# Key maxima rows transferred in step 7, query rows behind step 1's diagonal keys, the queries' bias sums behind the first convolution half

## The chip, the cores and the metric
The kernel runs on one core of a Trainium2 chip. The time is the device time of one execution in microseconds (us). TensorE (PE), VectorE (DVE), ScalarE (ACT) and GpSimd (POOL) run their own instruction streams and meet at semaphores; the sync engine (SP) issues nearly all the DMAs, in one queue and in the order of its program.

## The reference
One decoder layer on 8 sequences of 128 tokens with 128 channels, in float32:

```
x = x + attn1(layernorm(x))        # 16 heads of 8 channels; queries and keys pass a 3-tap
                                   # convolution and a projection of [input, convolved input];
                                   # scores * tau + delta, softmax over 128 keys, times V, out
x = x + attn2(layernorm(x), ctx, mask)   # 16 heads, keys and values from ctx, masked softmax
x = x + moe(layernorm(x))          # 64 experts, 8 of them per token, and one shared expert
```

In `attn1` the projection and the convolution are folded: `Q3 = conv(q_in) @ qp2 + q_in @ qp1` becomes one convolution over the normalised input, with a bias column that sums `qp2 @ convq_b` and three taps applied to the query bias. The same holds for the keys.

## The kernel before, in words
**Head.** The input is normalised (DVE), turned to channels-by-tokens on PE (`turn_inputs`, two halves of four sequences), copied to `xnT` by ACT, and convolved on PE (`convolve`, line 531, one half at a time). `sum_bias` (line 524) is eight small float32 matmuls with one output column: two passes each for four products. `sum_bias(0, ...)` (queries) stands between the two `turn_inputs`, `sum_bias(1, ...)` (keys) behind the first half's convolution. DVE applies the results in `foldb` (line 1240).

**Stacked operands.** The attention multiplies float32 numbers as two float32r parts, high and low. For each of 16 heads the parts are stacked on 32 partitions: rows 0 to 7 of such a block are for the running maximum (`S_MAX = 8`), rows 8 to 31 hold the eight channels times three parts. The stacked keys are `kst[0]` (first attention) and `kst[1]` (second), the stacked queries `qst`. Sequences 0 to 3 are stacked by PE (`stack`, line 495) and evicted by ACT and DVE. Sequences 4 to 7, and the keys of the second attention, go through DRAM: `put_rows(i, ...)` (line 376, three DMAs of 256 KB, or 512 KB for i = 2) stores the parts, `get_rows` (line 382, four DMAs) reads them back in stacked order. The maxima rows of the keys are constants: ACT writes them for sequences 4 to 7 of `kst[0]` (`fill_keys`, signal `kst_filled`), and `get_maxima(lo)` (line 388) copies them by four DMAs from `kst[0]` to `kst[1]`, 8 partitions to 8 partitions, 64 KB each. It is called for lo = 0 and lo = 4: eight DMAs, signal `maxima_got`.

**Steps.** There are 16 steps (`STEPS`), one for each sequence in each attention. In a step PE computes the scores of 16 heads in four groups against `kbd`, a block-diagonal copy of that sequence's keys with two buffers. DVE takes the maxima (`maximum`, line 1295) and splits them (`split_max`), PE turns them (`turn_max`, L656 and L659), ACT and DVE write `qbd`, PE computes the transposed scores, ACT the exponentials, PE the product with the values. PE runs one step ahead with `scores`. In steps 7 and 11 `scores(s + 1, 0)` stands late, between the groups of `scoresT(s)`, because the queries of the second attention are made there (`second_stack`).

**The SP queue** (lines 358 to 477). Behind the loads: wait for `kst_filled`, `get_maxima(0)` and `(4)`, wait for the split keys, `put_rows(0)`, wait for the split queries, `put_rows(1)`. Then a loop over s = 1 to 15: wait for the keys' source (`kst_ready`, `rows_got`; from s = 8 also `maxima_got`), wait until step s - 2's scores are read (`scored`), four DMAs that write `kbd` for step s (line 439), `move_rows(s)` (line 395: the `get_rows` of later sequences, `put_rows(2)` at s = 6, `get_rows(2)` at 7 and 9), and loads of expert weights (line 370; five of 192 KB at s = 8). POOL also waits for `maxima_got` before it splits the weights of pairs 5 to 9 (line 1846), behind step 7's exponentials.

Of the kernel before, what the change touches and what calls it, by code (L numbers as in the profile page):

```python
# [19 lines left out]
G = 4  # L20
# [10 lines left out]
Q_PARTS, K_PARTS = (0, 1, 0), (0, 0, 1)  # L31
# [30 lines left out]
def decoder_layer(nc, x, ctxT, mask, pack_a, pack_b, w3, rowsd, outT):  # L62
# [3 lines left out]
    with ExitStack() as ctx:  # L66
# [3 lines left out]
        def sem(name):  # L70
            return ctx.enter_context(nc.semaphore(name))
# [51 lines left out]
        qhl = by_part("qhl")  # L123
# [96 lines left out]
        qhi_ready = sem("qhi_ready")  # L220
        qlo_ready = sem("qlo_ready")
# [7 lines left out]
        kst_filled = sem("kst_filled")  # L229
# [105 lines left out]
        def wait(eng, signal, value):  # L335

            if not isinstance(value, int) or value > 0:
                eng.wait_ge(signal, value)
# [17 lines left out]
        @block.sync  # L356
        def _(sp):
            sp.dma_start(xres[:, :, :], x.rearrange("(b p) d -> p b d", p=P)).then_inc(ld_x, 16)
            nf = cols_a[FOLD_LAST][1]
            sp.dma_start(pa[:, 0:nf], pack_a[:, 0:nf]).then_inc(ld_f, 16)  # L360
            sp.dma_start(pa[:, nf:n_a], pack_a[:, nf:n_a]).then_inc(ld_a, 16)
            sp.dma_start(ctxs[:, :, :], ctxT.rearrange("p (b t) -> p b t", b=B)).then_inc(ld_ctx, 16)
            sp.dma_start(pb[:, :], pack_b).then_inc(ld_b, 16)
            sp.dma_start(masku[:, :, :], mask.rearrange("b q k -> q b k")).then_inc(ld_mask, 16)
            w3v = w3.rearrange("p (n m c) -> p n m c", m=3, c=P)
            def load(pair):

                if pair >= RING:
                    sp.wait_ge(wlo_ready, pair + 1 - RING)
                sp.dma_start(ring[:, pair % RING, :, :], w3v[:, pair, :, :]).then_inc(ld_w[pair % RING], 16)  # L370

            for pair in range(RING):
                load(pair)


            def put_rows(i, hl, first, parts):

                for m, a in enumerate(parts):
                    sp.dma_start(split_rows[i, :, m, P * first:T],  # L379
                                 hl[:, a, first:B, :].bitcast(F32).rearrange("p b t -> p (b t)")).then_inc(rows_put[i], 16)  # L380

            def get_rows(i, st, lo, hi, quarters):
                src = split_rows[i].rearrange("(g j d) m t -> j (d m) g t", g=G, j=J)
                for j in quarters:
                    sp.dma_start(st[32 * j + S_MAX:32 * j + 32, :, lo:hi, :].bitcast(F32).rearrange("p g b t -> p g (b t)"),
                                 src[j, :, :, P * lo:P * hi]).then_inc(rows_got[i][lo // 2], 16)

            def get_maxima(lo):

                for j in range(J):  # L390
                    sp.dma_start(kst[1][32 * j:32 * j + S_MAX, :, lo:lo + 4, :].bitcast(F32).rearrange("p g b t -> p g (b t)"),  # L391
                                 kst[0][32 * j:32 * j + S_MAX, :, 4:B, :].bitcast(F32).rearrange("p g b t -> p g (b t)"))\
                        .then_inc(maxima_got, 16)

            def move_rows(s):

                if s == 2:
                    sp.wait_ge(rows_put[0], 48)
                    get_rows(0, kst[0], 4, 6, range(J))
                if s == 3:  # L400
                    sp.wait_ge(rows_put[1], 48)
                    sp.wait_ge(qst_cleared, 1)
                    get_rows(1, qst, 4, 6, range(J))
                if s == 4:
                    get_rows(0, kst[0], 6, B, range(J))
                if s == 5:
                    get_rows(1, qst, 6, B, range(J))
                if s == 6:
                    sp.wait_ge(khi_ready, 4)
                    sp.wait_ge(klo_ready, 4)  # L410
                    put_rows(2, khl[1], 0, K_PARTS)
                if s == 7:
                    sp.wait_ge(rows_put[2], 48)
                    get_rows(2, kst[1], 0, 4, range(J))
                if s == 9:
                    get_rows(2, kst[1], 4, B, range(J))

            sp.wait_ge(kst_filled, G)
            get_maxima(0)
            get_maxima(4)  # L420
            sp.wait_ge(khi_ready, 2)
            sp.wait_ge(klo_ready, 2)
            put_rows(0, khl[0], 4, K_PARTS)
            sp.wait_ge(qhi_ready, 2)
            sp.wait_ge(qlo_ready, 2)
            put_rows(1, qhl, 4, Q_PARTS)
            sp.wait_ge(rows_ready, 3)
            for s in range(1, STEPS):
                n, b = s // B, s % B
                if s < 4:  # L430
                    sp.wait_ge(kst_ready, G)
                elif s < B:
                    sp.wait_ge(rows_got[0][2 if s < 6 else 3], 64)
                else:
                    sp.wait_ge(rows_got[2][b // 4 * 2], 64)
                    sp.wait_ge(maxima_got, 128)
                wait(sp, scored, G * (s - 1))
                for j in range(J):
                    sp.dma_start(kbd[32 * j:32 * j + 32, s % 2, :, j, :].bitcast(F32),
                                 kst[n][32 * j:32 * j + 32, :, b, :].bitcast(F32)).then_inc(kbd_ready[s % 2], 16)  # L440
                move_rows(s)
                for pair in PAIR_LOADS.get(s, ()):
                    load(pair)

            def coefficient_rows(n):

                c = n // PER_HALF
                sp.wait_ge(gate_scaled, n + 1 - ROWS)
                e0 = 2 * (n - PER_HALF * c) - 2
                for r in range(2):  # L450
                    sp.dma_start(spread[I * r:I * r + I, n % ROWS, :, :].rearrange("p b t -> p (b t)"),
                                 rowsd[c, e0 + r:e0 + r + 1, :].broadcast_to([I, HALF])).then_inc(ld_c[n % ROWS], 16)

            def rows_out(c):

                sp.wait_ge(rowsT_copied, c + 1)
                sp.dma_start(rowsd[c, :, :], coef_rows[:, c, :]).then_inc(rows_stored, 16)
                sp.wait_ge(rows_stored, 16 * (c + 1))

            load(EARLY_PAIRS + RING - 1)  # L460
            rows_out(0)
            for n in range(FIRST, UNITS):
                if n == PER_HALF + 1:
                    rows_out(1)
                if n != PER_HALF:
                    coefficient_rows(n)
                if n in load_unit:
                    load(load_unit[n])
                if n == PER_HALF + LAG + ROWS + 2:
                    sp.wait_ge(out_copied, 1)  # L470
                    sp.dma_start(outT[:, 0:HALF], outs[:, 0, :]).then_inc(stored, 16)

            for i in range(2):
                sp.wait_ge(out_copied, i + 2)
                cols = slice(2 * P * i, 2 * P * i + 2 * P)
                sp.dma_start(outT[:, HALF + 2 * P * i:HALF + 2 * P * i + 2 * P], outs[:, 1, cols]).then_inc(stored, 16)
            sp.wait_ge(stored, 48)
# [3 lines left out]
        def _(pe):  # L481
# [3 lines left out]
            def mm(out, lhsT, rhs, start=True, stop=True):  # L485
                return pe.matmul(out, lhsT, rhs, start=start, stop=stop)  # L486

            def turn_inputs(n, c, out):

                for b in range(4 * c, 4 * c + 4):  # L490
                    pe.wait_ge(xn_ready, B * n + b + 1)
                    last = pe.transpose(out[:, P * (b % 4):P * (b % 4) + P], xn[:, b, :], ident)  # L492
                last.then_inc(xT_done, 1)
# [30 lines left out]
            def sum_bias(n, proj, conv_bias, bias):  # L524

                mm(bank[4][:, n:n + 1], A(proj), A(conv_bias), True, False)
                for k in range(3):
                    last = mm(bank[4][:, n:n + 1], folds[n][:, k, :], A(bias), False, k == 2)
                last.then_inc(bias_summed, 1)
# [18 lines left out]
            pe.wait_ge(natural_copied, 1)  # L548
            compose(0)
            turn_inputs(0, 0, bank[0])  # L550
            sum_bias(0, "qp2T", "cqb", "bq")
            compose(1)
            turn_inputs(0, 1, bank[1])
            pe.wait_ge(pads_ready, 2)
# [1 line left out]
            for c in range(2):  # L556
                pe.wait_ge(xT_copied, c + 1)
                pe.wait_ge(compose_copied, c + 1)
                convolve(0, convq, c, bank[5 + c]).then_inc(q_done, 1)
                if c == 0:  # L560
                    sum_bias(1, "kp2T", "ckb", "bk")

            def time_scales():
# [1363 lines left out]
```

## Time and profile before

| | us |
|---|---|
| median of 3 runs | 304.18 (302.94 to 401.68) |
| the profiled execution | 303.79 |
| its span (first to last instruction) | 302.0 |
| PE busy | 288.7 (96%) |
| DVE, ACT, POOL busy | 228.2, 191.3, 185.3 |

The span is what the profiler covers; 1.8 us of the profiled execution lie around it. PE is busy nearly all the time, but a matmul's end is modelled, and a busy PE can run at half clock. The profile divides the span in 40 slices of 7.55 us. "L439" is line 439 of the kernel; SPq is a DMA issue on the sync engine; matmuls issued by a helper all have the helper's line, L486. A DMA share is the mean busy share of 16 DMA engines.

### The profile page before, as it was taken

What the parts mean: (1) busy time and instruction counts of PE and PEld (TensorE: products, weight loads), DVE (VectorE), ACT (ScalarE), POOL (GpSimd) and SP (SyncE); (2) the same over time, 40 slices, a digit from 0 to 9 for tenths busy, and PEclk for the clock granted to TensorE, in tenths of its full rate; (3) what the DMA queues carried; (4) which work ended last, traced back from release to release, by engine and by line L of the source; (5) the groups of instructions that cost most, each with busy time, mean ns of one, the idle gap of its engine ahead of it and who ended that gap; (6) DMA issues with size and microseconds to landing.
All of it is one profiled execution on the core that took longest, in us unless ns stands there. A gap on an engine that the chain in (4) does not pass through costs nothing.

```text
span 302.0 us, 5440 instructions
## 1 busy us (share of the span) xinstructions
PE 288.7 (96%) x1721; PEld 206.3 (68%) x1721; DVE 228.2 (76%) x513; ACT 191.3 (63%) x352; POOL 185.3 (61%) x259
## 2 busy tenths in 40 slices
PE   8999979999999999899889999999999999999995
PEld 3654756666655565456665788888888888888883
DVE  3698877799859886987896559789956676676664
ACT  2698827796884666466752797766655555555553
POOL 8430061098708870985177799999975666666661
PEclk9999968999999999999999999999999999999999
DMA  7702764457576243350000637766434353444311
GB/s 260 242 2 31 194 161 101 101 112 258 111 201 124 63 105 95 89 140 2 2 1 25 199 113 205 214 198 188 131 99 137 109 171 126 127 134 131 123 61 35
DMA packets 30636, 37.18 MB, mean 123 GB/s; under 512 B 5136, under 2 KB 19856, under 8 KB 30608
## 3 DMA queue, kind: packets, MB, share of 16 engines
q1 hardware_dynamic: 30608, 36.84, 43.0%
q8 instruction: 14, 0.23, 0.4%
q14 instruction: 14, 0.11, 0.1%
HBM read 28.43 MB, written 3.93 MB: 107 GB/s over the span
## 4 chain that ended last, share of the span: by engine, by line
PE 80%; DVE 10%; SPq 5%; ACT 2%; issue 2%; DMA 1%; ACTq 0%; DVEq 0%
PE bank L486 54%; PE bank L866 5%; PE bank L868 5%; PE bank L867 5%; PE bank L672 2%; SPq L391 2%; PE bank L647 2%; PE bank L690 2%; SPq L379 1%; PE bank L659 1%; DVE conv L1232 1%; DVE conv L1230 1%; PE bank L695 1%; PE bank L492 1%; PE bank L656 1%
## 5 line engine op out<-in xcount | busy, mean ns | idle before, releaser
L1864 POOL TENSOR_TENSOR qbd<-vs,qbd 128x512 fp32r<-128x512 f32 x65 | 83.8, 1291 | 33.3 <-ACT qbd L1175 33.2
L486 PE MATMUL bank<-khl,stacks 128*128 128x512 f32 x396 | 101.5, 392 | 1.9 <-DVE vs L1659 1.9
L486 PEld LDWEIGHTS bank<-khl,stacks 128*128 128x128 f32 x396 | 73.5, 188 | 18.7 <-issue 3.7
L1690 DVE TENSOR_TENSOR conv<-bank,conv 128x512 f32<-128x512 f32 x60 | 41.5, 692 | 31.4 <-ACT bank L1139 28.2
L1139 ACT ACTIVATE bank<-bank 128x512 f32<-128x512 f32 x61 | 35.5, 582 | 43.9 <-PE bank L486 43.9
L1298 DVE TENSOR_REDUCE rawmax<-bank 128x4 f32<-128x512 f32 x64 | 43.3, 684 | 10.9 <-PE bank L486 10.0
L1175 ACT ACTIVATE qbd<-vs 128x512 fp32r<-128x512 f32 x65 | 40.6, 624 | 7.1 <-DVE vs L1667 4.6
L486 PE MATMUL bank<-stacks 128*128 128x512 f32 x96 | 42.2, 488 | 2.8 <-DMA stacks<-stacks 2.0
L1698 DVE TENSOR_TENSOR vs<-conv,bank 128x512 f32<-128x512 f32 x61 | 41.9, 687 | 2.1
L1063 ACT ACTIVATE conv<-bank 128x512 f32<-128x512 f32 x64 | 35.1, 596 | 7.0 <-PE bank L486 6.3
L1828 POOL TENSOR_TENSOR stacks<-ring,stacks 128x384 fp32r<-128x384 f32 x33 | 33.6, 1020 | 1.4
L486 PE MATMUL bank<-qbd,stacks 128*128 128x512 f32 x64 | 30.7, 530 | 0.4 <-ACT conv L1063 0.4
L1072 ACT ACTIVATE qbd<-bank 32x512 fp32r<-32x512 f32 x40 | 23.5, 587 | 11.9 <-PE bank L659 11.6
L866 PE MATMUL bank<-qbd,stacks 128*128 128x512 f32 (+1 forms) x67 | 26.4, 394 | 0.7 <-POOL qbd L1864 0.6
L868 PE MATMUL bank<-qbd,stacks 128*128 128x512 f32 (+1 forms) x67 | 25.9, 386 | 0.0
L867 PE MATMUL bank<-qbd,stacks 128*128 128x512 f32 (+1 forms) x67 | 25.9, 386 | 0.0
L486 PEld LDWEIGHTS bank<-stacks 128*128 128x128 f32 x96 | 18.4, 196 | 8.2 <-DMA stacks<-stacks 2.3
L486 PE MATMUL bank<-conv,vs 128*9 128x128 f32 (+1 forms) x520 | 23.3, 279 | 0.0
L1051 ACT ACTIVATE oT<-bank 128x512 f32<-128x512 f32 x16 | 9.6, 598 | 15.1 <-PE bank L486 15.1
L1834 POOL CAST stacks<-ring 128x384 fp32r<-128x384 f32 x17 | 8.6, 504 | 17.0 <-ACT conv L1063 9.4
L1314 DVE CAST qbd<-bank 32x512 fp32r<-32x512 f32 x24 | 16.7, 694 | 1.6 <-PE bank L659 1.0
L486 PEld LDWEIGHTS bank<-conv,vs 128*9 128x9 f32 (+1 forms) x520 | 12.4, 91 | 7.6 <-issue 5.7
(239 smaller groups left out, 440.9 us busy)
## 6 DMA issues: line engine op xcount, KB each, us to landing
conv<-coefficient_rows SPq DMA_DIRECT2D x122, 128.0 KB, 2.9
ring<-w SPq DMA_DIRECT2D x33, 192.0 KB, 3.6
stacks<-stacks SPq DMA_DIRECT2D x68, 64.0 KB, 2.1
split_rows<-stacks SPq DMA_DIRECT2D x6, 256.0 KB, 3.4
stacks<-split_rows SPq DMA_DIRECT2D x16, 96.0 KB
split_rows<-khl SPq DMA_DIRECT2D x3, 512.0 KB, 4.3
stacks<-split_rows SPq DMA_DIRECT2D x8, 192.0 KB
pa<-pack_a SPq DMA_DIRECT2D x1, 706.0 KB, 5.4
```

Of the source, the lines that this page charges most:

```text
L486: return pe.matmul(out, lhsT, rhs, start=start, stop=stop)
L866: pe.matmul(acc, whi(pair)[:, 2, :], hhi[:, w, cols], start=False, stop=False, skip_group_check=True)
L867: pe.matmul(acc, whi(pair)[:, 2, :], hlo[:, w, cols], start=False, stop=False, skip_group_check=True)
L868: pe.matmul(acc, wlo(pair)[:, 2, :], hhi[:, w, cols], start=False, stop=stop, skip_group_check=True).then_inc(down_done, 1)
L1063: act.activation(probs[:, i % 8, :, :].rearrange("p j t -> p (j t)"), bank[2 + i % 2][:, :], ACT.Exp, scale=SCALE).then_inc(exped, 1)
L1139: act.activation(out, four(2 + p), ACT.Silu).then_inc(silu_done, 1)
L1175: act.activation(hhi[:, n % 4, :].rearrange("p (b t) -> p b t", b=4), hx[n % 4], ACT.Copy).then_inc(hhi_ready, 1)
L1298: dve.tensor_reduce(rawmax[:, s % 2, g, :].unsqueeze(2), bank[i % 2][:, :].rearrange("p (j k) -> p j k", j=J), AX.X, ALU.max, negate=True) ...
L1690: dve.tensor_tensor(out, gate, spread[:, n % ROWS, :, :], ALU.mult).then_inc(gate_scaled, 1)
L1698: dve.tensor_tensor(hx[n % 4], scaled[:, 4 * p:4 * p + 4, :], four(4 + p), ALU.mult).then_inc(h_done, 1)
L1828: pool.tensor_tensor(wlo(pair), ring[:, pair % RING, :, :], whi(pair).bitcast(F32), ALU.subtract).then_inc(wlo_ready, 1)
L1864: pool.tensor_tensor(hlo[:, n % 4, :].rearrange("p (b t) -> p b t", b=4), hx[n % 4], hhi[:, n % 4, :].bitcast(F32).rearrange("p (b t) -> p ...
```

## The change
It has three edits. The eight `get_maxima` DMAs, and the wait for `kst_filled` before them, move from the head of the SP queue into `move_rows(7)`, behind `get_rows(2, kst[1], 0, 4)`. `put_rows(1)` with its waits moves from before the loop to s = 1 of the loop, behind the four `kbd` DMAs. The queries' `sum_bias` moves from between the two input turns to behind the first half of the query convolution, in front of the keys' one.

```diff
@@ move_rows
                 if s == 7:
                     sp.wait_ge(rows_put[2], 48)
                     get_rows(2, kst[1], 0, 4, range(J))
+                    sp.wait_ge(kst_filled, G)
+                    get_maxima(0)
+                    get_maxima(4)
                 if s == 9:
                     get_rows(2, kst[1], 4, B, range(J))
 
-            sp.wait_ge(kst_filled, G)
-            get_maxima(0)
-            get_maxima(4)
             sp.wait_ge(khi_ready, 2)
             sp.wait_ge(klo_ready, 2)
             put_rows(0, khl[0], 4, K_PARTS)
-            sp.wait_ge(qhi_ready, 2)
-            sp.wait_ge(qlo_ready, 2)
-            put_rows(1, qhl, 4, Q_PARTS)
             sp.wait_ge(rows_ready, 3)
@@ loop over s
                                  kst[n][32 * j:32 * j + 32, :, b, :].bitcast(F32)).then_inc(kbd_ready[s % 2], 16)
+                if s == 1:
+                    sp.wait_ge(qhi_ready, 2)
+                    sp.wait_ge(qlo_ready, 2)
+                    put_rows(1, qhl, 4, Q_PARTS)
                 move_rows(s)
@@ tensor engine
             turn_inputs(0, 0, bank[0])
-            sum_bias(0, "qp2T", "cqb", "bq")
             compose(1)
             turn_inputs(0, 1, bank[1])
@@
                 convolve(0, convq, c, bank[5 + c]).then_inc(q_done, 1)
                 if c == 0:
+                    sum_bias(0, "qp2T", "cqb", "bq")
                     sum_bias(1, "kp2T", "ckb", "bk")
```

## Rows read from the trace of the kernel before
**Rows 1.** The page: busy us (share) xinstructions, and the clock in 40 slices.
```profile
PE 288.7 (96%) x1721; PEld 206.3 (68%) x1721; DVE 228.2 (76%) x513; ACT 191.3 (63%) x352; POOL 185.3 (61%) x259
...
PEclk9999968999999999999999999999999999999999
```
**Rows 2.** The chain of waits, 36 to 49 us: start, us, what.
```profile
36.87 1.11 SPq L439
...
39.41 2.09 DMA stacks<-stacks
```
**Rows 3.** Timeline, PE's: start, us, instruction, [idle before <-releaser].
```profile
41.54 0.79 PE L486 MATMUL bank<-stacks 128*128 128x512 f32 x1 [1.98 <-DMA stacks<-stacks]
```
**Rows 4.** Timeline of the SP queue.
```profile
24.86 7.18 SPq L391 DMA_DIRECT2D stacks<-stacks  x8
32.16 4.61 SPq L379 DMA_DIRECT2D split_rows<-stacks  x6
...
73.91 1.56 SPq L385 DMA_DIRECT2D stacks<-split_rows  x4
80.83 2.52 SPq L439 DMA_DIRECT2D stacks<-stacks  x4
83.40 2.51 SPq L370 DMA_DIRECT2D ring<-w  x5
86.02 2.54 SPq L439 DMA_DIRECT2D stacks<-stacks  x4
```
**Rows 5.** Timeline of DVE and ACT, 30 to 36 us.
```profile
30.21 0.75 DVE L1261 SCALAR_TENSOR_TENSOR stacks<-bank,foldb,stacks 128x512 fp32r<-128x512 f32 x1 [0.69 <-ACT stacks L970]
...
34.32 0.69 ACT L974 ACTIVATE stacks<-bank,key_rows 128x512 fp32r<-128x512 f32 x1 [0.23 <-PE bank L486]
```
**Rows 6.** Timeline of DVE, 40 to 49 us.
```profile
40.54 0.19 DVE L1306 TENSOR_TENSOR negmax<-rawmax,negmax 128x16 fp32r<-128x16 f32 x1
...
42.38 0.69 DVE L1298 TENSOR_REDUCE rawmax<-bank 128x4 f32<-128x512 f32 x1 [1.51 <-PE bank L486]
...
48.01 0.19 DVE L1306 TENSOR_TENSOR negmax<-rawmax,negmax 128x16 fp32r<-128x16 f32 x1
```
**Rows 7.** Timeline of PE, 8 to 30 us: a bias sum, the last convolution's end.
```profile
11.14 0.81 PE L486 MATMUL bank<-pa,qin 128*128 128x1 f32 x6
...
28.95 0.50 PE L537 MATMUL bank<-small,kin 128*128 128x4 f32 x4
```
**Rows 8.** Windows: us, busy (count) of PE, PEld, DVE, ACT, POOL, PEclk, DMA share, GB/s.
```profile
26.00:33.00 7.00, 7.00 (x24) 3.66 (x23) 5.67 (x10) 5.83 (x10) 0.00 (x0) 1.00 0.44 65
...
41.00:42.00 1.00, 0.46 (x1) 0.46 (x2) 0.00 (x0) 0.00 (x0) 1.00 (x1) 0.50 0.40 77
...
70.00:72.00 2.00, 2.00 (x11) 1.27 (x10) 1.61 (x7) 1.90 (x5) 1.45 (x7) 1.00 1.02 395
...
76.00:79.00 3.00, 3.00 (x23) 2.06 (x26) 2.55 (x8) 2.66 (x6) 2.29 (x8) 1.00 0.81 158
...
80.00:81.00 1.00, 1.00 (x19) 0.58 (x7) 0.93 (x5) 0.77 (x3) 0.92 (x2) 1.00 0.00 0
...
88.00:92.00 4.00, 3.88 (x19) 2.65 (x19) 3.22 (x7) 2.69 (x6) 0.64 (x2) 1.00 0.73 174
```
**Rows 9.** Line 439 in step 8's, step 9's and step 10's windows: landing times.
```profile
DMA to landing us min/median/max: 2.1/2.1/2.1
...
DMA to landing us min/median/max: 3.0/3.2/3.3
...
DMA to landing us min/median/max: 3.4/3.7/4.0
```
**Rows 10.** Timeline of PE: `scores(8, 0)`, `scores(9, 0)`, step 8's L659.
```profile
88.12 0.38 PE L647 MATMUL bank<-maskb,identb 128*128 128x512 bf16 x1
...
92.44 0.38 PE L647 MATMUL bank<-maskb,identb 128*128 128x512 bf16 x1 [0.36 <-DVE rawmax L1298]
...
93.62 0.51 PE L659 MATMUL bank<-identr,negmax 128*128 128x512 f32 x1 [0.33 <-DVE negmax L1306]
```

## The prediction
> **What bounds the kernel now.** I read the page first: PE is busy 96% of the span, so most of it is PE's own work, and the clock line has one dip, in slices 6 and 7 [rows 1]. The chain of waits for that place runs along the SP queue: eight maxima DMAs, six row stores, then the four `kbd` DMAs of step 1, the last issued at 39.41 and landed 2.09 later [rows 2, 4]. PE, which wants them for `scores(1, 0)`, has been idle for 1.98 us when it starts at 41.54, the one long wait for a DMA in the steps [rows 3]. At 41 us the granted clock is 0.50, that is 1.2 instead of 2.4 GHz [rows 8]. So the reader is to see two things: at 40 us the end is set by the SP queue, elsewhere (step 7 among it) by PE, with SP ahead of it by a margin that has to be read.
>
> **Part 1, the head of the SP queue.** Without the maxima, `put_rows(0)` can issue when the keys' low parts are there, at 30.21 + 0.75 = 30.96 [rows 5], not at 32.16 [rows 4]. Six such DMAs took 4.61 us, so even if most of that falls to these three, they end before 34.3. The `kbd` DMAs then wait for the last stacked keys: 34.32 + 0.69 = 35.01 [rows 5]. They issue at 35.05 instead of 36.87 and at 0.65 each the fourth starts at 37.0; with the observed 2.1 it lands at 39.1, at the slower pace seen (2.54 for three) at 39.7. The old date was 41.50. The supply is 1.8 to 2.4 us earlier.
>
> What is late next is DVE: step 0's maxima are split at 40.54 + 0.19 = 40.73 and nothing in the change touches them. Behind that DVE idled until 42.38, 1.51 us by the row [rows 6]. `scores(1, 0)` would now be ready by 40.2, so this maximum starts at 40.87 and the DVE chain to the next split (at 48.01 before, mostly without holes) moves up by 1.5, plus the 0.2 to 0.4 us of waits for PE in it that the full clock takes out. **Gain: 1.7 us.** Bounds: 0, if the stores in flight slow the four DMAs until 41.5, and 2.4, the whole advance of the supply; I take 1.7 because DVE's own row is nearest. The clock dip should vanish, as PE's hole shrinks from 1.98 to about 0.4 us, but it is worth little here since DVE bounds the stretch.
>
> **Part 2, `put_rows(1)`.** Its three issues (about 1.6 us) come behind step 1's four, 37.7 to 39.3. Behind them queue step 2's `kbd` DMAs, which waited for step 0's scores until about 39.5 anyway. Nothing. If one issue is as slow as the slowest seen, step 2's move by 1 us and are still before PE's next step, which waits for the second split (46.4 after part 1's gain). Its reader, `get_rows(1)`, comes two steps later.
>
> **Part 3, the bias sums.** They are 0.81 us and a bit of PE time [rows 7]. PE works without a hole from there to 29.45, where the last key convolution ends [rows 7], and DVE's low keys, which set the start of the stores and stacks, follow from it: DVE is idle for 0.69 before them [rows 5]. The sums stay within that stretch, so its end does not move; the second input half reaches ACT and DVE 0.8 us sooner, which they spend waiting for PE at its end. Cost and gain nothing; bounds plus or minus 0.8, the sum's own length, if a hole opens or closes.
>
> **Part 4, the maxima in step 7.** All times here are on the old clock; the gain of part 1 moves PE and SP alike. `get_rows(2)` issues from 73.91 to 75.47. Its traffic runs at a share of 0.81 and 158 GB/s and is gone at 80, and step 8's `kbd` DMAs start at 80.83 [rows 4, 8]: 1.0 us from the end of traffic to the next issue. The eight maxima DMAs issue from 75.5. In the old place they took long: first issue 24.86, a share of only 0.44 and 65 GB/s from 26 to 33, 455 of 524 KB by then, so their traffic ended about 34.0 at that pace [rows 4, 8]; a little less is likely, 33.6, as it began after 26. That is some 7.6 us of traffic for half a megabyte, where `put_rows(2)` had 395 GB/s at a share of 1.02 [rows 8]. They are limited by something of their own, and it is not the total rate (the packets are as long as those of the rows, 2 KB).
>
> Step 8 now waits for `maxima_got`. When does it come? Call T the start of step 8's `kbd` issues (80.83 before). If the maxima ran beside the rows with no loss: 75.5 + (33.6 - 24.86) + 1.0 = 85.2. If they run behind them, as step 10's DMAs did, which landed in 3.4 to 4.0 us behind a `get_rows` against 2.1 elsewhere [rows 9]: 79.8 + 6.5 to 7.6 + 1.0 = 87.3 to 88.4 (6.5 is the 7.6 at 0.44 packed to a share of 0.51, half of the full 1.02, about what these copies never passed). If both were spread over all engines with no loss, 0.81 x 4.5 and 0.44 x 7.6 us of work at 1.02 from 75.3 end at 82.1, T = 83.1. I take 87.3; the queueing seen in step 10 is the nearest row.
>
> The Trainium skill (DMA: Bandwidth & Descriptors, section "Why a DMA increments its semaphore by 16 and not by 1") says that a transfer from the sync engine runs on the largest number up to 16 that divides both sides' slowest dimension, and on the lowest-numbered engines: 8 for these 8 partitions. The trace agrees with a share of 0.44 while only the maxima move. By that rule the maxima share every one of their engines with the rows ahead of them, which gives the 87.3; were it wrong, T would be between 83.1 and 85.2.
>
> PE reads step 8's `kbd` at 88.12 [rows 10]. Of four DMAs the last starts 1.95 behind T and lands 2.1 later [rows 9], so T may be 84.07 at most. With T = 87.3 PE waits 3.2 us. Next, SP issues the five weight loads before step 9's `kbd`: their fourth starts at T + 7.15 and lands 3.0 later (it did behind the loads [rows 9]), at 97.45. PE wanted step 9's at 92.44 and could have taken them at 92.9, with L659 waiting for DVE until 93.62 [rows 10]; moved by 3.2 that is 96.1, so 1.3 us more are lost. The other possibility is that the 3.2 us hole brings the clock down, as the 1.98 us one did [rows 3, 8]: then PE's 3.88 busy us of 88 to 92 double, less what DVE's waits give back, 2.5 us, and step 9's wait is covered. One or the other, 1.3 or 2.5; I take the middle, 1.9, as one old hole is all there is to judge by. **Loss: 3.2 + 1.9 = 5.1 us.** POOL also waits for the maxima but was idle until 91.28 for step 7's exponentials. Step 10's DMAs come one step later, with no weight loads between, and SP has caught up by then.
>
> **Sum.** -1.7 + 0 + 0 + 5.1 = +3.4: 303.79 + 3.4 = **307.2 us**. The profiled execution is 0.4 below the median of three.
>
> **Rivals.**
> *The maxima run beside the rows.* T = 85.2: PE waits 1.1 at 88.12 and 1.3 more for step 9, each shorter than the hole that brought the clock down. -1.7 + 2.4 = +0.7: 304.5. For it: the share of 0.81 leaves room; against: 0.81 + 0.44 is more than 1.02, and step 10's landings.
> *The maxima are hidden.* The one that is not slower. Place: `maxima_got` at SP, s = 8; price nothing; it decides at T of about 82.8 (from there step 9's DMAs land by 92.9). It needs the spread of 83.1, or a faster pace than at the head, where DVE and ACT may have been what slowed the copies. With T = 83.1 the loss is 0.3, without any it is none: -1.4 to -1.7, 302.2. Against it: alone they took 9.7 us from first issue to landing, and here 8.0 are given.
> *Slower by over 2%.* T = 88.4 gives a wait of 4.3; the clock falls (2.5 more) and part 1 gives nothing for a slowed issue: 303.8 + 6.8 = 310.6.
> *The early part does not work* (step 1's DMAs still late by stores in flight) with the forecast's loss: 303.8 + 5.1 = 308.9; within the range.
>
> **How the numbers follow.** Two per cent is 6 us, about what a measurement here can tell from no change. Forecast with its neighbour 308.9: 0.53. Beside the rows, 304.5: 0.20. Hidden, 302.2: 0.17. Over 2% slower: 0.08. Over 2% faster needs 6 us where the whole supply gain is 2.4: 0.02. The range takes in the hidden case's value and the forecast with T = 88.4 or without part 1's gain, 302.0 to 309.6.
>
> **What would show it.** In the changed profile PE's wait for a DMA at 41.5 is gone and the clock line has no dip there; L391 stands at about 74; SP waits some 5 to 6 us at line 439 in step 8 and PE has a hole of about 3 us before the first L647, perhaps with a clock of 0.50 behind it. The forecast is wrong if the maxima's landing comes within 8 us of their first issue, or if their rate is well over the 65 GB/s of the head.

## Result: 1.6% slower, and the profile after

| | before | changed |
|---|---|---|
| median, us | 303.91 (4 runs) | 307.75 (4 runs, 307.54 to 310.2) |
| profiled execution, span | 302.0 | 306.0 |

The ratio of the changed kernel to the one before is 1.0156 [1.0087, 1.0224]; 307.2 was forecast. One of the four runs before took 401.68 us; the ratio is of the others, whose median is 303.64. The kernel is slower beyond the interval; a loss of over 2% is not excluded by it. In the two profiled executions the head gained 2.0 us and steps 8 and 9 lost 6.0.

The turned maxima of each step (L659 before, L660 in the changed kernel) serve as milestones: the difference of their starts shows where the time went, to 0.1 us:

| start of it in step | 0 | 1 | 7 | 8 | 9 |
|---|---|---|---|---|---|
| before | 42.56 | 48.26 | 84.08 | 93.62 | 100.06 |
| changed | 40.75 | 46.23 | 82.11 | 97.30 | 104.07 |
| difference | -1.81 | -2.03 | -1.97 | +3.68 | +4.01 |

The span's +4.0 is complete at step 9. Between steps 7 and 8 lie 15.19 us instead of 9.54: 5.65 lost; between 8 and 9 another 0.33.

The SP queue of the changed kernel, from its timeline (start, us, instruction); it answers to [rows 4]:

```profile
30.97 1.29 SPq L379 DMA_DIRECT2D split_rows<-stacks  x3
35.00 2.71 SPq L436 DMA_DIRECT2D stacks<-stacks  x4
37.81 1.52 SPq L379 DMA_DIRECT2D split_rows<-stacks  x3
...
71.36 1.99 SPq L385 DMA_DIRECT2D stacks<-split_rows  x4
73.40 6.96 SPq L391 DMA_DIRECT2D stacks<-stacks  x8
86.17 2.56 SPq L436 DMA_DIRECT2D stacks<-stacks  x4
88.77 2.51 SPq L370 DMA_DIRECT2D ring<-w  x5
91.40 2.54 SPq L436 DMA_DIRECT2D stacks<-stacks  x4
93.98 1.82 SPq L385 DMA_DIRECT2D stacks<-split_rows  x4
95.90 8.33 SPq L436 DMA_DIRECT2D stacks<-stacks  x8
```

The stores start at 30.97 and step 1's keys at 35.00, as worked out. The last maxima DMA is issued at 79.67, step 8's keys only at 86.17. The chain of waits says what stands between (the landing of that last copy), and that step 10's keys were late too:

```profile
79.67 6.44 DMA stacks<-stacks
...
97.82 5.51 DMA stacks<-stacks
```

PE at the three places, from its timeline; the first row answers to [rows 3], the others to [rows 10]:

```profile
39.76 0.77 PE L487 MATMUL bank<-stacks 128*128 128x512 f32 x1 [0.29 <-DVE rawmax L1299]
...
90.29 0.39 PE L648 MATMUL bank<-maskb,identb 128*128 128x512 bf16 x1 [4.28 <-DMA stacks<-stacks]
...
96.34 0.39 PE L648 MATMUL bank<-maskb,identb 128*128 128x512 bf16 x1 [0.54 <-DMA stacks<-stacks]
```

The wait at the head has become one for DVE; the 4.28 us is new. Windows (us, busy of PE, PEld, DVE, ACT, POOL, then clock, DMA share, GB/s), to read beside [rows 8]:

```profile
40.00:41.00 1.00, 1.00 (x3) 0.53 (x4) 0.93 (x5) 0.00 (x0) 0.18 (x1) 0.50 1.00 358
...
76.00:79.00 3.00, 3.00 (x41) 1.91 (x39) 2.87 (x7) 2.50 (x7) 2.42 (x7) 1.00 0.68 120
...
80.00:84.00 4.00, 3.67 (x30) 2.12 (x27) 1.95 (x7) 3.70 (x9) 0.00 (x0) 1.00 0.52 76
84.00:85.00 1.00, 1.00 (x19) 0.52 (x18) 0.90 (x4) 0.47 (x2) 0.00 (x0) 1.00 0.16 20
...
91.00:94.00 3.00, 3.00 (x8) 1.91 (x7) 1.46 (x3) 1.08 (x2) 0.00 (x0) 0.50 0.85 272
```

Once the rows are through, the maxima are alone from 80 to 84: a share of 0.52, 76 GB/s, against 0.44 and 65 at the head before. The first copy is issued at 73.40 and the last has landed at 86.11, 12.7 us later. At 40 us and again from 91 to 94 the clock is at 1.2 GHz.

### The profile page after: what moved, and what is told of

It is laid out like the page before. It is cut to its first block, busy times and chain, and to the rows that moved or that the text cites. A ratio compares the mean times of both kernels' runs of the same rounds, so it can differ in the third digit from the quotient of the medians.

```text
span 306.0 us, 5440 instructions
## 1 busy us (share of the span) xinstructions
PE 289.4 (95%) x1721; PEld 206.3 (67%) x1721; DVE 228.2 (75%) x513; ACT 191.5 (63%) x352; POOL 185.0 (60%) x259
## 4 chain that ended last, share of the span: by engine, by line
PE 71%; DVE 10%; SPq 7%; DMA 7%; issue 2%; ACT 1%; ACTq 0%; DVEq 0%
PE bank L487 48%; PE bank L867 5%; PE bank L869 5%; PE bank L868 5%; DMA stacks<-stacks 4%; SPq L436 3%; PE bank L673 2%; SPq L391 2%; PE bank L648 2%; DVE rawmax L1299 2%; DMA split_rows<-khl 2%; DMA xres<-x 1%; SPq L385 1%; PE bank L691 1%; PE bank L660 1%
## 5 line engine op out<-in xcount | busy, mean ns | idle before, releaser
L1176 ACT ACTIVATE qbd<-vs 128x512 fp32r<-128x512 f32 x65 | 40.7, 625 | 7.1 <-DVE vs L1668 4.6
L648 PE MATMUL bank<-maskb,identb 128*128 128x512 bf16 x32 | 12.7, 396 | 5.3 <-DMA stacks<-stacks 5.0
```

The costliest lines, as they stand in the source:

```text
L1176: act.activation(hhi[:, n % 4, :].rearrange("p (b t) -> p b t", b=4), hx[n % 4], ACT.Copy).then_inc(hhi_ready, 1)
```

## Experiments
Times are medians; "L659" and "L660" are the same matmul in kernels with other line numbers. Experiments 1 to 4, 5 to 8 and 9 to 12 were compared with runs of the kernel before of 303.67, 303.70 and 303.94; every ratio is to that kernel. The diffs are cut to the lines that matter, and some of their comments are not in the kernels. Those of 1, 2, 5, 7 and 8 start from the kernel before, that of 10 starts from experiment 9, of 11 from 4, of 12 from 6, and the others from the changed kernel.

### 1. The maxima's edit alone
```diff
-            sp.wait_ge(kst_filled, G); get_maxima(0); get_maxima(4)   # head of the queue
+                    # in move_rows(7), behind get_rows(2, kst[1], 0, 4)
+                    sp.wait_ge(kst_filled, G); get_maxima(0); get_maxima(4)
```


> The kernel before with the maxima's edit alone: their eight DMAs stand in step 7, the query stores and the bias sum stay where they were. My theory (in step 7 the maxima run behind the row reads, and step 8's key DMAs wait for them) puts the whole loss into this edit, and also the gain at the head: six stores fit between 30.97 and 35.0, so step 1's key DMAs still issue at 35.1 to 35.6. It expects the changed kernel's time, 307.3 to 308.2, a wait of 4 us on PE at 90 us, and L379 x6 ending by 35.6. The rival (the query stores' move carries the head's gain) expects 309 to 310: the loss of 6 without the gain of 2.

308.67, ratio 1.0164 [1.0151, 1.0177]. Loss and head gain are both in this edit: L659 of step 1 stands at 46.27, that of step 8 at 98.65. The six stores were issued by 34.1, in time. It is 0.5 above what I gave, since more is lost at step 8 than in the changed kernel: 7.1 us instead of 5.65. Experiment 9 comes back to that.

### 2. The other two edits, maxima at the head
```diff
             sp.wait_ge(kst_filled, G)
             get_maxima(0)
             get_maxima(4)
             put_rows(0, khl[0], 4, K_PARTS)
-            put_rows(1, qhl, 4, Q_PARTS)
+            # put_rows(1, ...) at s = 1 behind the kbd DMAs; sum_bias(0, ...) behind convolve(0, ..., 0)
```


> The other two edits without the maxima's: maxima stay at the head of the SP queue, the query stores stand behind step 1's key DMAs, the bias sum behind the first convolution half. My theory expects no loss at all at step 8, and a gain at the head, since step 1's key DMAs now issue behind three stores instead of six: at 35.1, 1.8 us sooner than in the kernel before, landing at 39.2 to 40.2. PE's second split moves up by 1.3 to 2.0: 301.9 to 302.6. A rival (the stores' traffic, now in front of step 2's DMAs, costs something or the gain needs the maxima gone, whose traffic still slows the three stores) expects 303.3 to 304.5.

302.09, ratio 0.9963 [0.9947, 0.998]. No loss at step 8 (L660 of steps 7 and 8 are 9.54 apart, as before), and by the times the gain is there. But the runs are of two kinds: eight at 301.66 to 302.27 and four at 303.5 to 303.74. The profile caught one of the latter, and its windows show why:

```profile
14.00:18.00 4.00, 4.00 (x26) 3.04 (x25) 3.56 (x3) 4.00 (x6) 3.99 (x2) 1.00 0.00 0
18.00:21.00 3.00, 3.00 (x5) 1.05 (x4) 2.93 (x6) 2.71 (x4) 0.00 (x0) 0.50 0.03 5
```

From 18 to 21 us PE runs at 1.2 GHz in the middle of the convolutions, with no hole before; what stands before are the two bias sums in a row, eight products of one column each, here 15.1 to 17.0:

```profile
15.12 0.36 PE L487 MATMUL bank<-pa 128*128 128x1 f32 x2
15.34 0.81 PE L487 MATMUL bank<-pa,qin 128*128 128x1 f32 x6
16.01 0.36 PE L487 MATMUL bank<-pa 128*128 128x1 f32 x2
16.24 0.81 PE L487 MATMUL bank<-pa,kin 128*128 128x1 f32 x6
16.91 4.37 PE L487 MATMUL bank<-xnT,oT 128*128 128x512 f32 x6
```

The last row took 2.82 us in the profile of the changed kernel. Step 1's L660 stands at 48.10 instead of 46.23, 1.9 us later.

### 3. The maxima spread over steps 2 to 5
```diff
                 move_rows(s)
+                if s == 2:
+                    sp.wait_ge(kst_filled, G)
+                if 2 <= s < 6:
+                    get_maxima(4 * (s // 4), range(2 * (s % 2), 2 * (s % 2) + 2))
```


> The changed kernel with the eight maxima DMAs in pairs behind the moves of steps 2, 3, 4 and 5 instead of all in step 7. My theory (the loss is only the place: behind the row reads, with 8 us to the wait) expects all maxima landed before 62 us, the SP wait in step 8 back to that for the rows, no PE wait at 88, and the head's gain kept: 301.7 to 302.6. A rival (these copies are slow wherever they stand, and delay the key DMAs queued behind them on the same DMA engines) expects PE waits for a DMA in steps 3 to 6 of together 1 to 3 us: 303 to 305.

306.25 over twelve runs (303.95 to 308.69); ratio, without the two longest (308.64 and 308.69), 1.0077 [1.0052, 1.0103]. My theory fell here, the rival was nearer, though by another mechanism. The SP queue itself became the bound of these steps:

```profile
59.50 1.48 SPq L391 DMA_DIRECT2D stacks<-stacks  x2
61.08 3.15 SPq L433 DMA_DIRECT2D stacks<-stacks  x4
64.27 1.82 SPq L385 DMA_DIRECT2D stacks<-split_rows  x4
66.13 1.48 SPq L391 DMA_DIRECT2D stacks<-stacks  x2
67.71 2.95 SPq L433 DMA_DIRECT2D stacks<-stacks  x4
```

One round takes 6.63 us (59.50 to 66.13) where PE's step takes 6.09, and the key DMAs behind maxima issue at 3.15 instead of 2.52. But from step 1's maxima to step 7's it is only 0.7 us longer than the changed kernel. The profile (306.1) shows two more losses. It has the slow head of experiment 2, 2.1 us at step 1's maxima. And the queue is still late when the copies are through: step 8's keys issue at 84.23, 0.7 us ahead of step 7's maxima, where it was 3.25 before, and PE waits for the keys of steps 9 and 10:

```profile
94.25 0.39 PE L649 MATMUL bank<-maskb,identb 128*128 128x512 bf16 x1 [1.31 <-DMA stacks<-stacks]
...
101.59 0.39 PE L649 MATMUL bank<-maskb,identb 128*128 128x512 bf16 x1 [0.82 <-DMA stacks<-stacks]
```

### 4. The maxima copied by POOL
```diff
+            pool.wait_ge(kst_filled, G)
+            for lo in (0, 4):
+                pool.tensor_copy(kst[1][:, :, lo:lo + 4, :]..., kst[0][:, :, 4:B, :]...).then_inc(maxima_got, 1)
             pool.wait_ge(kbd_first, 1)
```


> The changed kernel without maxima DMAs: POOL copies the constants from the first stacked keys to the second in two instructions of 128x2048, behind ACT's fill at about 25 us, where it was idle until 37. SP waits for them at step 2 and step 7, POOL as before. By its casts of 128x384 in 0.50 us, 2.7 us each, so done by 30.5. My theory expects what the spread one does, and no queue effects: 301.7 to 302.4. The rival (POOL beside DVE slows DVE's long operations between 25 and 31, which set the low parts) expects the stores at 31.5 to 33 instead of 30.97 and 302.5 to 304.

303.97 (303.71 to 305.77), ratio 1.0013 [1.0001, 1.0024]. Step 8 is as before, but the head lost what was gained. The profile is of the slowest of the twelve runs (305.77), so it overstates the loss. DVE beside the copies (24.22 to 28.39 on POOL):

```profile
24.71 1.91 DVE L1243 CAST identb<-pa 128x128 bf16<-128x128 f32 x1
26.55 1.92 DVE L1244 CAST identr<-pa 128x128 fp32r<-128x128 f32 x1
```

Each of these took 0.22 before. DVE then keeps PE waiting for its low keys by 2.1 us, and behind that wait the clock is 0.50 from 34 to 37.

### 5. The copies twice as wide
```diff
-kst[1][32 * j:32 * j + S_MAX, :, lo:lo + 4, :]        kst[0][32 * j:32 * j + S_MAX, :, 4:B, :]
+kst[1][32 * j:32 * j + 2 * S_MAX, :, lo:lo + 4, :]    kst[0][32 * j:32 * j + 2 * S_MAX, :, 4:B, :]
```


> The kernel before with its eight maxima DMAs, at the head, made twice as wide: 16 partitions to 16 instead of 8 to 8, 128 KB each (the eight extra rows are overwritten later by the row reads; SP waits for the copies at step 2). My theory (a copy of 8 partitions is carried by half of the DMA engines, one of 16 by all) expects the same time for twice the bytes: eight issues in about 7 us, a share of 0.85 to 0.95 and 130 to 150 GB/s from 26 to 33 us, against 0.44 and 65. The rival (the copies are limited by something that does not depend on the number of partitions, such as the issue or the memory port they read) expects 65 to 80 GB/s, a share near 0.5 and issues that stretch to 12 to 14 us.

One run, 303.33 (SP also waits for the copies at step 2). Twice the bytes in the same time:

```profile
24.68 7.22 SPq L391 DMA_DIRECT2D stacks<-stacks  x8
```
```profile
26.00:33.00 7.00, 7.00 (x23) 3.69 (x22) 5.65 (x10) 5.81 (x10) 0.00 (x0) 1.00 0.91 129
```

A share of 0.91 and 129 GB/s against 0.44 and 65 [rows 8]. By the share, the narrow copy keeps half of the DMA engines busy. It does not show why each engine carries only 8 to 9 GB/s (65 over half of 16) where the stores reach 25 (395 over 16): the number of ports that 16 partitions reach doubled too.

### 6. Half of the maxima in step 7
```diff
                     get_rows(2, kst[1], 0, 4, range(J))
                     sp.wait_ge(kst_filled, G)
                     get_maxima(0)
-                    get_maxima(4)       # now at the head, and sum_bias(0, ...) in its old place
```


> The changed kernel with the bias sum in its old place and only four of the eight maxima DMAs in step 7; the other four stand at the head of the SP queue. The queue theory expects the copies' landing to scale with their number: 0.9 us of traffic each behind the row reads, so step 8's key DMAs issue at 82.4 to 83.0 instead of 86.2, PE waits 0.3 to 1.0 at step 8 and up to 1.3 at step 9, the clock stays at 1.00 there, and the time is 303.2 to 304.4. The rival (the wait for one more semaphore behind the rows costs a fixed amount, whatever the number) expects a PE wait of 3 us or more and 306 or more.

305.88, ratio 1.0078 [1.0058, 1.0097]. Step 8's keys issue at 82.86, in the range given, and PE waits 0.91 for them. So the delay scales with the number of copies: four fewer, 3.3 us sooner, or 2.9 against experiment 9 (85.71), which has the bias sum in the same place; with none in step 7 they issue at 79.19 (experiment 8). The time missed, for what I had declared covered: PE waits 2.25 for step 9's keys and, behind a get_rows, for step 10's. The columns of the landing line of step 10's keys here, and of experiment 12's, are min/median/max from issue:

```profile
DMA to landing us min/median/max: 4.7/6.1/6.8
```

### 7. The bias sum's move alone
```diff
-            sum_bias(0, "qp2T", "cqb", "bq")      # between the two turn_inputs
+                    sum_bias(0, "qp2T", "cqb", "bq")   # behind convolve(0, convq, 0, ...)
                     sum_bias(1, "kp2T", "ckb", "bk")
```


> The kernel before with the bias sum's move alone: the queries' eight one-column matmul passes stand directly in front of the keys' eight. The prediction had nothing for it, 303.4 to 304.1 in every run. The theory formed from the second experiment's trace (16 one-column passes in a row sometimes bring the granted clock to 0.50 for 3.4 us behind them, and the convolutions there run at half speed) expects runs of two kinds: some at 303.4 to 304.0, some 1.7 to 2.0 us above, and a median between 303.7 and 305.6.

303.04 (302.15 to 303.91), ratio 0.9978 [0.9966, 0.9991]. A gain, which neither had: ACT fills the keys 1.0 us sooner, so the maxima, still at the head, issue from 23.88 instead of 24.86, the stores from 31.20 instead of 32.16 and step 1's keys from 36.48 instead of 36.87. The runs spread over 1.8 us, where the kernel before spreads over 1.3, without a gap between two kinds. But they part by their mean clock over the whole execution: five with 0.992 to 1.00 took 302.15 to 302.69, six with 0.987 to 0.989 took 303.04 to 303.91. The profile (302.15) is of the first sort, with no dip of the clock at 40 us. So the gain is largest in executions that are spared a long dip, and how much of it is the earlier keys themselves is not separated.

### 8. The query stores' move alone
```diff
-            sp.wait_ge(qhi_ready, 2)
-            sp.wait_ge(qlo_ready, 2)
-            put_rows(1, qhl, 4, Q_PARTS)
@@ for s in range(1, STEPS): behind the kbd DMAs
+                if s == 1:
+                    sp.wait_ge(qhi_ready, 2)
+                    sp.wait_ge(qlo_ready, 2)
+                    put_rows(1, qhl, 4, Q_PARTS)
```


> The kernel before with the query stores' move alone; maxima at the head, bias sum in its old place. It is the second experiment without the bias edit. If that experiment's gain came from the stores and its two kinds of runs from the bias sum, this one gives 301.7 to 302.4 in all runs, with no value near 303.6, and the clock line is 1.00 up to 38 us. The rival (the second kind of run comes from the stores' place, or from nothing in the kernel) expects values near 303.6 in some runs again.

**301.84** (301.48 to 302.25, 5 runs), ratio 0.9941 [0.9928, 0.9954]: the fastest of all, 1.9% below the changed kernel. Step 1's keys issue behind three stores:

```profile
24.74 7.27 SPq L391 DMA_DIRECT2D stacks<-stacks  x8
32.13 2.85 SPq L379 DMA_DIRECT2D split_rows<-stacks  x3
35.08 2.62 SPq L436 DMA_DIRECT2D stacks<-stacks  x4
37.80 1.54 SPq L379 DMA_DIRECT2D split_rows<-stacks  x3
```
```profile
18.00:21.00 3.00, 3.00 (x11) 1.58 (x10) 2.96 (x5) 2.71 (x3) 0.00 (x0) 1.00 0.00 0
...
38.00:48.00 10.00, 8.31 (x53) 5.32 (x52) 9.74 (x25) 5.92 (x12) 5.67 (x4) 1.00 0.70 181
```

No run near 303.6, and the clock is 1.00 throughout. Together with 2, where the bias sum is the only difference, this points at the bias sum's place for the slow head. Five runs alone would be few (it came in four of twelve); experiments 11 and 12, also with the old place, have 21 more, and none of the three spreads over more than 0.8 us.

### 9. The changed kernel, bias sum in its old place
```diff
             turn_inputs(0, 0, bank[0])
+            sum_bias(0, "qp2T", "cqb", "bq")
```


> The changed kernel with the bias sum back between the two input turns. My theory: the head's gain and step 8's loss are both of the SP queue, so nothing changes but the occasional slower head: 307.3 to 308.3, with L660 of steps 7 and 8 more than 15 us apart as in the changed kernel (9.5 before). The rival (the bias edit carries a part of the changed kernel's time) expects a difference of more than 0.7 us from it in the runs of the faster kind.

308.93, ratio 1.0168 [1.0155, 1.0181], 1.2 above the changed kernel; the expectation was too low. The head is the same (L660 of step 1 at 46.47, of step 7 at 82.17), step 8's at 98.64. What differs between the two profiles is the length of the slow clock. It falls at 88.7, still inside PE's wait, and holds to 95.5; in the changed kernel it falls at 90.9, behind the wait, and holds to 94.3. Two of this profile's windows:

```profile
88.00:89.00 1.00, 0.00 (x0) 0.00 (x0) 0.00 (x0) 0.00 (x0) 0.00 (x0) 0.83 0.41 79
...
94.00:95.00 1.00, 1.00 (x6) 0.85 (x5) 0.59 (x1) 0.60 (x1) 0.01 (x1) 0.50 0.45 100
```

PE waits for no DMA at step 9 then, but for DVE; in this profile the slow clock alone carries it past 96. The profile of experiment 1, also without the bias sum's move, has the same picture and the same time. That the bias sum's place decides it is not shown. The mean clocks of the runs speak against the clock as the whole cause: the one run here with 0.989 took 308.86, no less than those with 0.983, and the changed kernel's fastest run (307.54) has 0.983. By the means, the kernel before has two lengths too: in its profile the clock is at 0.50 from 40.7 to 47.5, a mean of 0.989, and others of its runs have a mean of 0.994, about half of that. Where the 1.2 us come from stays open.

### 10. PE kept busy in its wait
```diff
+                if s == B and g == 0:
+                    pe.wait_ge(maxed, i - 1)
+                    for _ in range(18):      # into the bank that scores(8, 0) overwrites
+                        pe.matmul(bank[0]..., identb[:, :], maskb[:, b, :]..., start=True, stop=True)
```


> The kernel of the ninth experiment with 18 matmuls of 128x512 put in front of the scores of step 8, into the bank that these scores overwrite: they fill PE's wait of 4.3 us, so that the granted clock should stay 1.00 behind it. The prediction's view (the clock's fall costs 1 to 1.5 us of the loss) expects the time to fall by that, to 306.0 to 306.8. The theory formed since (step 9's key DMAs, which land at 96.3 in the changed kernel whatever PE does, bound the stretch, so the clock was covered) expects no more than 0.3 us, 307.2 to 308.2, and a longer wait for a DMA in front of step 9's scores, 1.5 to 2.2 us instead of 0.5.

308.64 (307.48 to 311.33), ratio 1.0175 [1.0137, 1.0213]. The clock holds at 1.00 until 96, and little is gained (0.3 of 308.93, inside the spread): PE stands before step 9's scores instead, longer than either theory had.

```profile
85.71 4.06 PE L638 MATMUL bank<-maskb,identb 128*128 128x512 bf16 x18
...
98.28 0.61 PE L653 MATMUL bank<-maskb,identb 128*128 128x512 bf16 x1 [4.42 <-DMA stacks<-stacks]
```

The last of step 9's key DMAs, issued at 92.92, landed 5.31 us later, against at most 3.3 in the changed kernel, so the profiled run (311.3), the second slowest of six, overstates this wait; the best (307.48) is at the time that my theory gave. What is shown is that the prediction's 306.0 to 306.8 was not reached in any run, and that in the profiled one the DMAs bound this stretch with a full clock as well.

### 11. The POOL copies without the casts beside them
```diff
+            dve.tensor_copy(identb[:, :], ident)   # both casts now before later_taps(0), at 12.6 us
+            dve.tensor_copy(identr[:, :], ident)
```


> The fourth experiment's copies on POOL, with the bias sum in its old place and DVE's two small casts (identb, identr, 0.22 us each in the kernel before, 1.9 us each beside the POOL copies) moved in front of the taps, to 13 us, where DVE idles. If the fourth experiment lost its 2 us by those two casts standing beside the copies, DVE is at its low keys by 25.8 again, the stores issue at 31 and the time is 301.6 to 302.4. The rival (the copies slow whatever DVE does beside them) expects operations of DVE between 24 and 29 us that are longer than in the kernel before (1.28, 0.75 and 0.43 us) and 303 or more.

303.22, ratio 0.9977 [0.9968, 0.9987]. Better than 4 by 0.75, but the rival holds: the scaling of tau now stands beside the copies and took 0.43 before, while L1271, which reads one operand from PSUM, keeps its 0.75.

```profile
26.45 1.08 DVE L1269 TENSOR_SCALAR tauT<-tauT 128x512 f32<-128x512 f32 x1 [0.29 <-issue]
27.57 0.75 DVE L1271 SCALAR_TENSOR_TENSOR qc<-bank,foldb,tauT 128x512 f32<-128x512 f32 x1
28.24 1.33 DVE L1269 TENSOR_SCALAR tauT<-tauT 128x512 f32<-128x512 f32 x1
```

The Trainium skill (SBUF — State Buffer, section "Who interferes with whom") says that copies, casts and tensor_scalar can take a second port pair which DVE shares with GpSimd, held for a whole instruction while the other blocks. The trace agrees: 0.22 became 1.9 beside POOL instructions of 2.1 us, and of DVE's operations beside them only casts and tensor_scalar stretched.

### 12. Half of the maxima, later row reads behind step 10's keys
```diff
-                if s == 9:
+                if s == 10:
                     get_rows(2, kst[1], 4, B, range(J))
```


> The sixth experiment (four maxima DMAs in step 7) with the later row reads, get_rows(2) for sequences 4 to 7, in step 10 instead of 9, behind step 10's key DMAs instead of in front. In the sixth, PE waited 0.9, 2.25 and 1.6 us for the key DMAs of steps 8, 9 and 10, the last of which landed 4.7 to 6.8 us after their issue. The theory that these queue behind the row reads on the DMA engines expects step 10's to land in 2.1 to 3.2 us, the third wait gone, the first two as they were: 304.0 to 304.8 against 305.9. The rival (SP's issue time is what is late) expects the landing times of step 10 as they were and 305.4 or more.

303.78 against 305.88 in experiment 6, a little below the 304.0 to 304.8 expected; ratio 0.9996 [0.9987, 1.0005]. The waits are now 1.28 and 1.70, and the third (1.60) is gone; step 10's keys land in:

```profile
DMA to landing us min/median/max: 2.1/2.1/3.8
```

So those keys were late because they queue behind row reads on the DMA engines. That SP now issues them sooner is not the whole of it, since the landing time counts from the issue.

## Why the prediction was right, step by step
**Part 1, the head: right, a little small.** 1.7 was forecast, 2.03 measured at step 1. The chain named (SP, then DVE's split) is the one in the trace. One claim fell: the clock's dip stayed, though it lasts from 39.7 to 43.1 instead of 40.7 to 47.5. It is 0.50 at 40 to 41 although PE's hole shrank to 0.29, and it is absent in the profiles of experiments 7, 8, 10, 11 and 12. It costs little, as was said, since DVE bounds the stretch: L660 of step 1 is at 46.23 with it and 46.06 without it (8), and the runs of experiment 12 take 303.65 to 303.93 with a mean clock of 1.00 and 303.6 to 304.33 with 0.994.

**A part of it was read wrongly.** The sum gave the gain to the maxima's removal. Experiment 8 has it all, and more surely, with the maxima where they were: either three stores fewer or eight copies fewer in front of step 1's keys is enough, because these wait for the last stacked keys at 35.0 anyway. With the forecast's own rows that could have been seen: 32.16 plus half of 4.61 is 34.5.

**Part 2: right.** Nothing behind the stores waits.

**Part 3, nothing: not quite.** The sum looked at PE's work and left out that the key fill comes sooner. Alone the move gains 0.7 (7). In experiment 2 it costs 1.6 (1.9 in the profile) in four runs of twelve, by the clock behind the one-column products. The changed kernel's run at 310.2 may be such a one; no profile shows it, and its mean clock, 0.989, is that of the profiled run.

**Part 4, the loss: right in kind, 6.0 instead of 5.1.** The mechanism is the one forecast: step 8's keys wait for the copies, the copies' traffic ends behind that of the row reads (alone from 80 to 84), and PE waits for the keys. T was put at 87.3; measured it is 86.17 plus the 1.97 gained, 88.1, at the late end of the bounds. The traffic had fallen off by 84.5, which is 86.5 on the old clock and inside the forecast's 86.3 to 87.4, but step 8's keys issued 1.7 later, not 1.0. PE's wait was 4.28 for 3.2; the rest, 1.7, is near the 1.9 forecast. That 1.9 was the middle of two possibilities, so its fit is partly luck. Behind the wait came what the prediction had as one or the other, a late step 9 or a slow clock, and it was both: 0.54 of waiting after a slow stretch. Experiment 10 shows the DMAs binding it with a full clock, the profile of 9 a longer slow stretch that binds it without them. The claim on step 10 ("SP has caught up by then") was wrong: step 9 is 0.33 us longer in the changed kernel, of which PE's row shows 0.15 as a wait for step 10's keys, and 6 has a whole wait of 1.60, for the row reads in front of those keys (12).

**The sum.** The span grew by 4.0, forecast 3.4. The two misses, 0.3 more gain and 0.9 more loss, partly cancel, so the total is nearer than its larger term.

**The rivals.** That the copies run beside the rows and that they are hidden both fall with the chain's 6.44 us and with experiment 6. The rule on the number of DMA engines (the Trainium skill, DMA: Bandwidth & Descriptors, "Why a DMA increments its semaphore by 16 and not by 1") is borne out by the share of 0.52 for 8 partitions and 0.91 for 16. One number of the rivals does not come out of the forecast's rows: it gives the copies 8.0 us, but from 75.5 to 82.8, where that rival decides, it is 7.3, which speaks against the rival a little more.

## What to carry to other kernels
A queue's idle stretch is the cheapest place for a transfer that nobody needs soon: the maxima stood in one at the head, and taking them out made nothing faster that reordering the three stores behind them did not. When a transfer moves to where another is awaited, count the traffic on the engines it uses, not bytes over the peak rate, and follow the queue for two more steps. Test the edits of a change one by one: here the stores' move alone brings the whole gain, and the maxima's place loses three times as much.

## What was not expected of the hardware
- The clock can fall with no hole in PE's work: after 16 passes of one column (1.9 us) it was 0.50 for 3.4 us, from 18.0 (2) and from 17.2 us (3), and 1.00 in other profiles with the same order (4, 7, the changed kernel).
- Nearly the same hole, 4.28 and 3.74 us, was followed by a slow stretch of 3.4 us (changed) or 6.8 us (9), and a hole of 1.98 us in the kernel before by one of 6.8. What decides the length stays open.
- A DMA's landing depends on what is queued behind it too, perhaps: 5.31 us for the last of four with row reads issued directly after it (10), 3.3 in the changed kernel with the same order. This stays open.
- What limits one DMA engine to 9 GB/s in the narrow copies stays open as well; experiment 5 changed engines and ports together. The Trainium skill (SBUF — State Buffer, section "Door 1: The DMA port swizzle") gives 27.2 GB/s for a port, and by its table 8 such partitions reach two, an estimate of 54 GB/s. The 65 to 76 measured are over that, with copies of different quarters in flight at once; no run here separates the ports from the engines.
